# First group's weights split from their tiles, two DMA queues, new homes for the first tiles

## What is computed

```
s = attn(xn)
g = silu(xn @ W.T + bias + sum_n 2*lw[n] * (xn @ A[n].T) @ B[n].T)
out = x + s * g
```

## Time and profile before

| | us |
|---|---|
| median of 3 runs (2731.54 to 2734.3) | 2731.64 |
| the profiled execution | 2726.47 |
| its span, first to last instruction | 2724.6 |
| TensorE busy (matmuls) | 2591.6 |
| ScalarE / GpSimd / VectorE busy | 1769.1 / 1726.9 / 1648.0 |
| mean granted clock of TensorE | 0.985 |

### The profile page before, as it was taken

How to read it: one execution, slowest core, us unless ns; L and a number is a source line. 1 busy time by engine, 2 the same in 40 slices (tenths; PEclk the granted TensorE clock), 3 DMA queues, 4 the chain that set the end, 5 groups by cost and what they waited for, 6 DMA issues and landing times.

```text
span 2724.6 us, 39884 instructions
## 1 busy us (share of the span) xinstructions
PE 2591.6 (95%) x13840; PEld 2296.2 (84%) x13840; DVE 1648.0 (60%) x3520; ACT 1769.1 (65%) x4627; POOL 1726.9 (63%) x845
## 2 busy tenths in 40 slices
PE   2759999999999999999999999999999999999997
PEld 2648888888888888888888888888888888888886
DVE  4536655656667656566566665557566756555656
ACT  2246666666866766766776676666776667667763
POOL 2467787886667665656576666566565856656553
PEclk8879999999999999999999999999999999999999
DMA  7777778877345333433335433433334433433323
GB/s 234 261 263 262 251 249 274 266 257 247 118 149 166 117 122 111 142 113 103 119 94 175 149 109 115 141 110 111 109 107 142 165 122 99 122 117 109 116 69 128
DMA packets 183095, 424.48 MB, mean 156 GB/s; under 512 B 33520, under 2 KB 74608, under 8 KB 182000
## 3 DMA queue, kind: packets, MB, share of 16 engines
q1 hardware_dynamic: 182896, 421.93, 48.1%
HBM read 349.51 MB, written 89.13 MB: 161 GB/s over the span
## 4 chain that ended last, share of the span: by engine, by line
PE 88%; DVE 3%; ACT 2%; POOL 2%; DMA 2%; issue 1%; SPq 1%; POOLq 0%; DVEq 0%; ACTq 0%
PE proj L488 21%; PE proj L490 21%; PE proj L489 21%; PE tr L581 5%; PE sc L488 3%; PE sc L489 3%; PE sc L490 3%; PE ot L489 3%; PE tr L561 3%; PE ot L490 3%; PE ot L488 3%; POOL wl L926 1%; PE tr L554 1%; DVE acc L1166 0%; ACT prob L781 0%
## 5 line engine op out<-in xcount | busy, mean ns | idle before, releaser
L926 POOL TENSOR_TENSOR wl<-wl,wh 128x896 fp32r<-128x896 f32 x448 | 977.4, 2209 | 614.3 <-ACT wh L707 614.1
L488 PE MATMUL proj<-wh,xh 128*128 128x448 f32 x1792 | 674.0, 376 | 53.8 <-POOL wl L926 50.1
L489 PE MATMUL proj<-wl,xh 128*128 128x448 f32 x1792 | 661.2, 369 | 0.0
L490 PE MATMUL proj<-wh,xl 128*128 128x448 f32 x1792 | 661.1, 369 | 0.0
L937 POOL TENSOR_TENSOR wb_lo<-wb_lo,wb_hi 128x1024 fp32r<-128x1024 f32 x128 | 307.1, 2400 | 311.3 <-ACT wb_hi L717 311.3
L774 ACT ACTIVATE prob<-prob,negmax 128x128 f32<-128x128 f32 (+3 forms) x512 | 286.8, 565 | 250.3 <-DVE negmax L1144 250.3
L707 ACT ACTIVATE wh<-wl 128x896 fp32r<-128x896 f32 x448 | 406.3, 966 | 56.7 <-DMA wl<-wu 56.2
L488 PE MATMUL proj<-o_hi,wb_hi 128*128 128x512 f32 x1024 | 424.7, 415 | 9.2 <-issue 6.1
L1166 DVE TENSOR_TENSOR acc<-acc,proj 128x512 f32<-128x512 f32 x480 | 327.1, 683 | 156.6 <-PE proj L490 155.2
L753 ACT ACTIVATE pT_hi<-tr 128x512 fp32r<-128x512 f32 (+3 forms) x512 | 197.5, 440 | 334.8 <-PE tr L581 334.7
L488 PEld LDWEIGHTS proj<-wh,xh 128*128 128x128 f32 x1792 | 339.4, 189 | 86.7 <-issue 50.6
(11 more groups left out here) (121 smaller groups left out, 4339.3 us busy)
## 6 DMA issues: line engine op xcount, KB each, us to landing
wl<-wu SPq DMA_DIRECT2D x448, 448.0 KB, 3.9
wb_lo<-wo_in SPq DMA_DIRECT2D x128, 512.0 KB, 3.3
wu<-xtok SPq DMA_DIRECT2D x14, 1792.0 KB, 10.1
wo_in<-wo SPq DMA_DIRECT2D x32, 512.0 KB, 5.8
xtok<-wa SPq DMA_DIRECT2D x56, 256.0 KB, 4.4
wu<-xtok SPq DMA_DIRECT2D x14, 896.0 KB, 5.9
gate_dram<-z_buf SPq DMA_DIRECT2D x32, 256.0 KB, 5.1
xtok<-wa SPq DMA_DIRECT2D x56, 128.0 KB, 4.4
```

What stands on the lines that cost most here:

```text
L488: pe.matmul(out, hi_l, hi_r, start=first, stop=False, skip_group_check=onto)
L489: pe.matmul(out, hi_l, lo_r, start=False, stop=False, skip_group_check=onto)
L490: return pe.matmul(out, lo_l, hi_r, start=False, stop=last, skip_group_check=onto)
L926: pool.tensor_tensor(w_slot(wl, w), w_slot(wl, w, True), w_slot(wh, w), ALU.subtract).then_inc(w_ready, 1)
```

## The change

- **Group 0 without memory.** ScalarE splits P1, P2, P6, P7, P4 and P5 straight from the prepared tiles (`split_first`), VectorE makes the low parts of P1, P2, P6 and GpSimd those of P7, P4, P5 (`low_first`, same name on both). Only P3 is still read from `wu`. The gate's 128 columns come into the tiles by eight ScalarE copies (`gate_columns`), and not from memory. The stores to `wu` stay, for the later sequences.
- **Two queues.** ScalarE issues LoRA's A and B, the identity, lw, slopes, q and k norm weights and the bias vector: 15 DMAs. SP starts with x. The bias vector has a semaphore of its own.
- **Other places.** `prob`, `bias_sb`, `z_buf`, `e_buf` and `rel_sb` become parts of one tensor `misc`. It holds the tile (0, 1) and before that raw LoRA; W's rows of the first half lie in `raw` and the end of `acc`, those of the second in `xtok`; the tile (1, 0) lies in `acc`, (1, 1) in `xtok`.
- **Order.** The statistics stand ahead of LoRA's scaling; pieces of P1 and P2 stand between the turns of x; two merges follow each piece of P6 and P7. `weight_sums` of (1, 0) and (1, 1) stand in VectorE's step (0, 0); before, VectorE made (1, 0) ahead of P3 and GpSimd (1, 1) ahead of (1, P1). A wait for the sums of (1, 0) stands before the first use of `acc` as the output's sum.

```diff
+DIRECT = 2 * P3
+ON_DVE = 2 * P7
...
+        def prep_place(g, h):
+            if (g, h) == (0, 1):
+                return misc[:]
+            return flat(acc if (g, h) in ((0, 0), (1, 0)) else xtok)
         def prep_tile(g, h, a, c):
+            at = 2 * a + c
+            return prep_place(g, h)[:, at * 896:at * 896 + 896].rearrange("p (k n) -> p k n", k=2)
+        def wt_slot(half, k):
+            if half == 1:
+                return flat(xtok)[:, 512 * k:512 * k + 512]
+            return flat(raw)[:, 512 * k:512 * k + 512] if k < 7 else flat(acc)[:, 3584:4096]
+        lora_a_raw, lora_b_raw = misc[:, 0:TILE], misc[:, TILE:2 * TILE]
...
-                sp.wait_ge(prep_in[h], 192 * (g + 1))
-                place = flat(xtok if g > 0 else raw if h else acc)
+                sp.wait_ge(prep_in[h], 192 * (g + 1) - 64)
+                if g == 0:
+                    sp.wait_ge(gate_cols, NK)
+                place = prep_place(g, h)
...
-            sp.dma_start(lora_a_raw, lora_a).then_inc(lora_in[0], 16)
-            sp.dma_start(lora_b_raw, lora_bt).then_inc(lora_in[1], 16)
-            for n in range(8):
-                sp.dma_start(lw_sb[16 * n:16 * n + 16, :],
-                             lw[n:n + 1, :].to_broadcast([16, 1])).then_inc(lw_in, 16)
-            sp.dma_start(xtok[:, 0, :], x_first[:, 0, :]).then_inc(x0_in[0], 16)
-            sp.dma_start(ident_sb[:], ident).then_inc(ident_in, 16)
-            for t in range(1, NT):
+            for t in range(NT):
                 sp.dma_start(xtok[:, t, :], x_first[:, t, :]).then_inc(x0_in[t], 16)
             load_gate_rows(0)
-            for dst, src in ((slope[:, 0:G], slopes), (qw_sb[:], qw), (kw_sb[:], kw)):
-                sp.dma_start(dst, src).then_inc(const_in, 16)
-            sp.dma_start(fb[:], ffn_b).then_inc(lw_in, 16)
             load_weights(0, 0)
             sp.wait_ge(lora_ready, 2)
             load_weights(0, 1)
-            store_gate_rows(0, range(NK))
-            sp.wait_ge(weff_out, 16 * NK)
-            for h in range(2):
-                load_gate_weights(0, h)
+            store_gate_rows(0)
             store_halves(0, 0)
             store_halves(0, 1)
-            load_product(0, P1)
-            load_product(0, P2)
+            sp.wait_ge(tr_done, TR["x", 0, 2 * NP - 1] + 1)
             load_gate_rows(1)
+            store_sums(0, 0)
             store_sums(0, 1)
-            store_sums(0, 0)
-            load_product(0, P6)
-            sp.wait_ge(tr_done, TR["x", 0, 2 * NP - 1] + 1)
+            store_gate_rows(1)
+            sp.wait_ge(weff_out[0], 16 * NK)
+            sp.wait_ge(prep_tst[0], 16)
+            sp.wait_ge(w_ready, 2 * P5 + 1 - ON_DVE)
             load_weights(1, 0)
             load_gate_weights(1, 0)
-            load_product(0, P7)
-            store_gate_rows(1, range(4))
-            load_product(0, P4)
-            store_halves(1, 0)
-            store_gate_rows(1, range(4, NK))
-            copy_b(0)
-            load_product(0, P5)
-            sp.wait_ge(weff_out, 32 * NK)
+            sp.wait_ge(prep_tst[1], 16)
+            sp.wait_ge(w_ready, 2 * P5 + 2 - ON_DVE)
             sp.dma_start(rel_sb[:], rel).then_inc(rel_in, 16)
             load_product(0, P3)
-            store_sums(1, 0)
-            sp.wait_ge(prep_tst[0], 16 * 2)
+            store_halves(1, 0)
+            copy_b(0)
+            sp.wait_ge(weff_out[1], 16 * NK)
             load_weights(1, 1)
             load_gate_weights(1, 1)
+            load_w(HW)
             store_halves(1, 1)
-            load_product(1, P1)
+            load_w(HW + 1)
             load_product(1, P2)
+            store_sums(1, 0)
...
-            for f in range(4, 2 * NP):
+            for f in range(4, 7):
                 turn_x(("x", 0, f))
-            for p in range(NP):
+            for i, (p, t) in enumerate(((P1, 0), (P1, 1), (P2, 0), (P2, 1))):
+                piece(0, p, t)
+                if i < 3:
+                    turn_x(("x", 0, 7 + i))
+            for f in range(10, 2 * NP):
+                turn_x(("x", 0, f))
+            for i, (p, t) in enumerate(((P6, 0), (P6, 1), (P7, 0), (P7, 1))):
+                piece(0, p, t)
+                merge_gate(1, 2 * i)
+                merge_gate(1, 2 * i + 1)
+            for p in (P4, P5, P3):
                 for t in range(2):
                     piece(0, p, t)
-                    if 2 * p + t < NK:
-                        merge_gate(1, 2 * p + t)
...
+            def split_first(p):
+                a, c = {P1: (0, 0), P2: (1, 0), P6: (1, 1), P7: (0, 1), P4: (1, 0), P5: (0, 0)}[p]
+                for h in range(2):
+                    w = 2 * p + h
+                    if p in (P1, P2):
+                        act.wait_ge(prep_in[h], 128)
+                        act.wait_ge(gate_cols, NK)
+                    else:
+                        act.wait_ge(prep_t[h], 4 if p in (P4, P5) else 3)
+                        if h == 0:
+                            act.wait_ge(w_half, p - 1)
+                        else:
+                            act.wait_ge(u_done, u_count(0, p - 2, 1))
+                    act.activation(wh[:, w % 4], prep_tile(0, h, a, c), ACT.Copy).then_inc(w_hi_done, 1)
+            def gate_columns(k):
+                a, h, i = k // 4, k % 4 // 2, k % 2
+                act.wait_ge(weff_ready, k + 1)
+                at = 2 * a * 896 + i * HALF + 384
+                dst = prep_place(0, h)[:, at:at + 1024].rearrange("p (c n) -> p c n", c=2)[:, :, 0:64]
+                act.activation(dst, wt_slot(0, k)[:, 0:P].rearrange("p (c n) -> p c n", c=2), ACT.Copy
+                               ).then_inc(gate_cols, 1)
...
             act.wait_ge(lora_in[0], 16)
             act.activation(lora_a_hi, lora_a_raw, ACT.Copy).then_inc(lora_hi, 1)
+            ln_rsqrt(0)
+            ln_scale(0, 0)
+            ln_scale(0, 1)
             act.wait_ge(lora_scaled, 1)
             act.activation(lora_b_hi, lora_b_raw, ACT.Copy).then_inc(lora_hi, 1)
-            ln_rsqrt(0)
-            for t in range(NT):
-                ln_scale(0, t)
-            for f in range(2 * NP):
+            ln_scale(0, 2)
+            ln_scale(0, 3)
+            for f in range(4):
                 x_hi(("x", 0, f))
-            act.wait_ge(qkw_ready, 1)
-            act.wait_ge(lw_in, 16 * 9)
-            split_product(0, P1)
-            split_product(0, P2)
-            act.wait_ge(prep_tst[1], 16)
-            for p in (P1, P2):
-                for t in range(2):
-                    take_piece(0, p, t)
-            split_product(0, P6)
+            for k in range(NK):
+                gate_columns(k)
+            split_first(P1)
+            for f in range(4, 7):
+                x_hi(("x", 0, f))
+            split_first(P2)
+            act.wait_ge(weff_out[0], 16 * NK)
+            for i, (p, t) in enumerate(((P1, 0), (P1, 1), (P2, 0), (P2, 1))):
+                take_piece(0, p, t)
+                if i < 3:
+                    x_hi(("x", 0, 7 + i))
+            for f in range(10, 2 * NP):
+                x_hi(("x", 0, f))
+            split_first(P6)
             for t in range(2):
                 square_rows(0, P2, t)
-            split_product(0, P7)
-            split_product(0, P4)
-            split_product(0, P5)
+            split_first(P7)
+            act.wait_ge(qkw_ready, 1)
+            act.wait_ge(fb_in, 16)
+            split_first(P4)
+            split_first(P5)
...
-            low_product(0, P1)
-            low_product(0, P2)
-            for p in (P6, P7, P4, P5, P3):
-                low_product(0, p)
+            low_first(P7)
+            low_first(P4)
+            low_first(P5)
+            low_product(0, P3)
             pool.wait_ge(rel_in, 16)
             bias_of(0)
-            weight_sums(1, 1)
             low_product(1, P1)
             low_product(1, P2)
...
             dve.memset(eps_sb[:], HD * RMS_EPS)
+            ln_stats(0, range(NT))
             dve.wait_ge(lora_in[1], 16)
-            dve.wait_ge(lw_in, 16 * 9)
+            dve.wait_ge(lw_in, 16 * 8)
             dve.tensor_scalar(lora_b_raw, lora_b_raw, lw_sb[:, 0:1], LORA_SCALE, ALU.mult, ALU.mult
                               ).then_inc(lora_scaled, 1)
-            ln_stats(0, range(NT))
+            ln_factors(0)
-            ln_factors(0)
             for f in range(4):
                 x_lo(("x", 0, f))
             for k in range(NK):
                 merge_gate(0, k)
-            for f in range(4, 2 * NP):
+            low_first(P1)
+            for f in range(4, 7):
                 x_lo(("x", 0, f))
-            weight_sums(0, 1)
-            weight_sums(0, 0)
-            for k in range(4):
-                merge_gate(1, k)
+            low_first(P2)
+            x_lo(("x", 0, 7))
+            for p in (P5, P7, P6):
+                weight_sum(0, 0, p)
+            x_lo(("x", 0, 8))
+            weight_sum(0, 1, P5)
+            x_lo(("x", 0, 9))
+            weight_sum(0, 1, P7)
```

(14 more changed lines are left out.)

70 lines of the change are left out of this document (46 added, 24 removed).

## The result

| | before | after |
|---|---|---|
| time, median (lowest to highest, runs) | 2731.59 us (2731.45 to 2734.3, 4) | 2691.47 us (2687.46 to 2694.81, 4) |
| profiled execution, its span | 2726.47, 2724.6 us | 2691.18, 2689.4 us |
| TensorE busy in the span | 2591.6 us, 95% | 2591.1 us, 96% |
| TensorE idle, 0 to 220 us | 98.4 us | 62.9 us |
| exponentials of head 0 / head 1 begin | 158.44 / 180.59 us | 111.89 / 142.60 us |

The account below looks back on a forecast made before the run. TensorE idles 98.4 us before 220 us, its big waits being round trips through memory, and bounds the kernel afterwards. Lead 42 takes the profiled 2726.47 to 2684.5; 5.2 more for the median gives 2689.6 us, range 2675 to 2707.

Parts of the forecast that it names:

- (a): Opening: x tiles first, small and LoRA transfers on a second queue; row scaling from 16.0 to 21.7 us, lead 12.4.
- (b): Group 0's gate rows and first weights without memory: low parts end at 35.5 and 38.0, P1 starts 35.6, lead 31.
- (c): P1, P2, P6, P7 with turns and merges: 36.7 us, last merge at 73.0; P4, P5 end at 82.6.
- (d): Group 1's halves loaded from 73.6 and 84.0: exponentials of head 0 begin at 108.7, lead 50.
- (e): Given back: group 1's sums, moved behind head 0's exponentials, delay their store to 123.9; head 1 at 138.3, lead 42.
- (f): From 220 us on TensorE is the bound, so the lead stays: profiled execution 2684.5, median 2689.6 us.
- Rival 2: Lead given back between 220 and 500 us, preparation of later groups being a second chain: 2711 us, chance 0.06.
- Rival 1: VectorE and GpSimd block each other all along, group 1's eight sums 23.2 instead of 10.2: 2703 us, chance 0.12.
- signs that I had named: Leads of 50 and 42 at heads 0 and 1, span shorter by the second, TensorE idle about 56, unchanged group means.
- rival 3: New addresses slow operations everywhere: at 1.6% the lead is used up, at 3% 2768 us; chance 0.02.
- rival 4: Gate columns or a store wait hold P1, group 0 keeps its old pace to 66.8: 2713 us, chance 0.05.
- rival 5: Memory quicker than counted: x at 9.5, no queueing in (d), no blocking: 2679 us, chance 0.15.

Follow-up runs that it names:

- e1: Changed kernel with all 15 small and LoRA transfers back on SyncE's queue behind the x tiles: 2689.79 us, ratio 0.9854.
- e2: Changed kernel with group 0's P1 and P2 weights read back from memory again, low parts still on VectorE: 2702.11 us, ratio 0.9901.
- e5: Changed kernel with GpSimd's x sums of P6, P5 and P3 held until VectorE made P1's two first low parts: 2692.11 us, ratio 0.9873.
- e3: Changed kernel with group 0's P4 and P5 weights from memory, their low parts on GpSimd: 2695.83 us, ratio 0.9873.
- e4: Changed kernel with group 1's sums in their old places, (1,0) on VectorE before P3, (1,1) on GpSimd before (1,P1): 2681.95 us, ratio 0.9823.
- e6: Changed kernel with head 0's exponentials on ScalarE between the splits of (1,P1,h0) and (1,P1,h1): 2683.59 us, ratio 0.984.
- e12: e9 with ScalarE's qT_hi and normalising for head 0 also ahead of the splits of (1,P1,h1) and (1,P2): 2676.73 us, ratio 0.9807.
- e9: Changed kernel with the edits of e5 and e6, plus the sums of (1,0) on VectorE ahead of P3: 2683.13 us, ratio 0.9821.
- e10: Changed kernel with GpSimd's 128x896 low parts of weights made in two instructions of 128x448 each: 2709.6 us, ratio 0.9916.

## Why the prediction was right

**(a)** Forecast 16.0 to 21.7 for the row scaling; measured 16.11 to 21.70. The second queue was right at nothing (e1).

**(b)** Low parts forecast to end at 35.5 and 38.0 with blocking, measured 35.62 and 38.82; P1 at 35.6, measured 35.77. e2 shows what one trip is worth, 9 us at both heads. e5 shows the blocking, 3.2 us on these two operations. That P1 came within 0.2 us is in part luck: in runs with the same instructions up to there it starts anywhere from 33.68 to 35.77, by TensorE's clock at the first merges (e5).

**(c)** The eight pieces and their stores took 2.6 us longer: the last merge left VectorE at 74.85 and not 73.0, SyncE spent 1.25 us on the issue of its store, and group 1's load went out at 76.23, not 73.6. That is the larger part of the 3.2 us by which step (d) ends late. That P4 and P5 cost nothing by either path was only implied there; e3 gives 3 us.

**(d)** Mis-sized, by what (c) handed on and by the first landing. From load to landed I took 8.8 us; it was 76.23 to 86.19, 10.0. The second half left at 87.86 and not 84.0, took 12.7 us (12.5 forecast) and was there at 100.53. From the second store to the exponentials I took 11.8 and it was 11.0, so they came at 111.89, not at 108.7: lead 46.5 and not 50.

**(e)** The mechanism was right and was the important one: the sums at 114.29 take 6.2 us (forecast 6 from 111.0), the last four end at 128.1 (123.8), and the store leaves 4.2 us late. 3.2 of that came from (d), and most of the other 1.0 from the scalings between the sums, which took 2.31 us (1.29 undisturbed, at 81.82). Head 1 is 4.3 us late, at 142.60 and not at 138.3, so from the store on the sum held: 14.5 us against 14.4. Its parts did not quite: P6's second tile, forecast to land 11.3 us behind the store, was there 10.4 behind it, at 138.48, and from there to the exponentials it took 4.1 and not 3.1, because P7's tiles land one by one (splits at 139.93 and 141.75), where I let their splits follow at once. Lead 38.0, not 42. e4 confirms what the moved sums cost.

TensorE's new stop was forecast at the right place, but the first and larger part of it has another cause than the one I named. Three of the turned probabilities' four high parts were made at 125.00, ahead of P6's split. The 8.70 us up to 132.45 are a wait for their low parts, which stand on VectorE behind the four sums and the gate's reciprocals (3.39 us at 128.46). Only the 4.69 us up to 140.18 hang on the fourth high part, at 139.34 behind P6's splits. So the moved sums hold head 1 by a second path too. The path by the store ended last: the exponentials of head 1 begin with no idle time before them, right behind P7's last split.

**(f)** "The lead stays" failed by 2.7 us: from 38.0 at head 1 it goes to 35.8 at head 8, up to 39.4 at head 14, back to 36.2 at head 16, and ends at 35.3. Rival 2's effect is there in small, by another mechanism: not a second chain, but VectorE's scaling meeting GpSimd's subtraction. Rival 1 too was partly right: the two block each other, at P1 and at single places later, not all along; the eight sums took 10.5 us and not 23.2.

**The sum.** That the total came within 1.9 us is luck: two errors cancel. The profiled executions differ by 35.3 us, not by 42; and I set the median 5.2 above the profiled execution as before, while here it is 0.3 above (2691.18 and 2691.47). The medians differ by 40.1. With the measured 35.3 and the distance I assumed, the sum is 2696.4, still inside the range. By the signs that I had named, the leads differ from 50 and 42 by 3.5 and 4.0 us, the span shortened by 7 us less than the second lead, and the idle time up to 220 us fell to 62.9 and not to 56: the mechanism held, and what missed were sizes, together 7.0 us: (c) by 2.6, (d) by 0.6, (e) by 1.1 and (f) by 2.7, all to the same side. Means of TensorE's groups didn't change, so rival 3 falls; rival 4 falls with P1 at 35.77, and rival 5 with the blocking and with the 12.7 us of the second half.

What stays open: which of two operations that begin within hundredths of a us is held. In after a scaling began 0.02 us behind the subtraction (340.06 and 340.04) and took its normal 0.68. There it was GpSimd that gave way, and more cheaply: its pair of subtractions took 5.23 us, where the pair in e5 that held up a scaling took 4.61.

## What to carry to other kernels

A round trip through memory on the path to an engine's first work is paid nearly in full (e2: 11.5 us at P1, 9 at the heads, 10 in the span); look for data that an earlier stage still has on chip. When a trip is removed, the work put in other places decides what is left of the gain: here about 9 of 44 us in the profiled executions went to eight sums that stood behind a busy engine's later work (e4), and ScalarE's order (what waits for a landing ahead of what is ready) kept head 1 back by 6.9 us by itself (e6), and by 7.3 once more (e12 against e9). In an engine that works in order, put what is ready ahead of what still has to land; and before judging an edit by 2 us of total time, read the lead stage by stage, since chance meetings downstream move it by more.

## What the runs showed of the hardware

- VectorE and GpSimd, both with operands in SBUF: 2.10 and 3.27 us against 1.09 and 1.08 with the neighbour held back; GpSimd 3.11 and 2.35. A hold lasts until the neighbour's instruction ends (0.68 becomes 2.63 beside 2.2 us, 1.13 beside 1.2 us), and in e10, with GpSimd's low parts in halves, one scaling was held in every group between 200 and 1000 us.
- A wait of 1.7 us in a TensorE that is otherwise full was followed by some 3 us at the lower clock (starts 0.33 instead of 0.17 us apart, granted clock 0.54 from 340.0 to 343.3 us in e5), so it cost about twice its length, 3.5 us.
- A second queue, on ScalarE, carrying LoRA and 13 small transfers beside the x tiles kept their statistics back to 13.77 us, where one queue with the x tiles first had them through at 10.16; the rows' scaling began 1.1 us earlier with one queue, and the times can't be told apart.
